# Three extra 128x512 products per round behind the key transposes of a graph-attention pass

## What is computed

```python
def _gat_conv(x, src, dst, W, a_src, a_dst, b, n_nodes):
    h = x @ W
    e = (h @ a_src)[src] + (h @ a_dst)[dst]
    e = jnp.where(e > 0, e, NEG_SLOPE * e)
    w = jnp.exp(e - e_max[dst])
    alpha = w / (denom[dst] + EPS)
    out = jax.ops.segment_sum(alpha[:, None] * h[src], dst, num_segments=n_nodes)
    return out + b
...
for m in range(3):
    x = x + jax.nn.sigmoid(_gat_conv(x, src, dst, Ws[m], att_src[m], att_dst[m], bias[m], n))
```

## Time and profile before

| | us |
|---|---|
| median of 3 runs | 12837.08 |
| lowest and highest of them | 12827.12 and 12846.73 |
| profiled execution, its time | 12854.73 |
| profiled execution, its span | 12853.1 |
| mean granted TensorE clock over the span | 0.735 |

### The profile page before, as it was taken

How to read it: one execution, slowest core, us unless ns; L and a number is a source line. 1 busy time by engine, 2 the same in 40 slices (tenths; PEclk the granted TensorE clock), 3 DMA queues, 4 the chain that set the end, 5 groups by cost and what they waited for, 6 DMA issues and landing times.

```text
span 12853.1 us, 167790 instructions
## 1 busy us (share of the span) xinstructions
PE 7017.4 (55%) x35048; PEld 5096.5 (40%) x35048; DVE 5349.2 (42%) x23215; ACT 4324.3 (34%) x9423; POOL 6444.5 (50%) x5862
## 2 busy tenths in 40 slices
PE   5666666750277007732222377774336887444888
PEld 2333335640266006621111255553224555333666
DVE  5666666651366226643333344441112333111544
ACT  5666663320133005532222244441113444111444
POOL 6666663456555656665666432335663333665000
PEclk9888887875688558855555688985557898555999
DMA  4555554445443555556666665666666777444998
GB/s 154 173 176 172 172 178 121 129 133 189 159 129 127 178 182 167 169 145 157 152 153 153 172 203 202 206 202 173 153 153 190 230 233 224 69 59 87 276 274 270
DMA packets 2016182, 2199.58 MB, mean 171 GB/s; under 512 B 235717, under 2 KB 1404889, under 8 KB 2009712
## 3 DMA queue, kind: packets, MB, share of 16 engines
q1 hardware_dynamic: 1698698, 1822.96, 43.4%
q0 software_dynamic: 308896, 372.55, 14.7%
q10 hardware_dynamic: 8390, 2.21, 0.1%
HBM read 1093.42 MB, written 1119.97 MB: 172 GB/s over the span
## 4 chain that ended last, share of the span: by engine, by line
DMA 18%; issue 11%; PE 10%; DVE 6%; another core or an unknown queue 5%; SPq 3%; POOL 2%; ACT 1%; POOLq 0%; DVEq 0%; ACTq 0%
DMA agg_d<-dO,fOI 11%; PE ps L1407 5%; DMA bXd<-agg_d 4%; PE ps L1394 2%; PE ps L1384 2%; DMA agg_d<-dO,dOI 2%; DMA aX<-y_d 2%; POOL bO L902 1%; SPq L653 1%; DVE aO L2004 1%; DVE uBS L1895 1%; DVE bXd L1977 1%; POOL agg_d L893 1%; PE ps L1382 1%
## 5 line engine op out<-in xcount | busy, mean ns | idle before, releaser
L954 POOL DMA_INDIRECT bXs<-x_d,fGI x784 | 794.7, 1014 | 1546.4 <-DMA x_d<-aH 1334.4
L893 POOL DMA_INDIRECT agg_d<-dO,fOI x784 | 1211.0, 1545 | 648.2 <-ACT dO L1082 417.7
L1082 ACT COPY dO<-ps 128x128 f32<-128x128 f32 (+1 forms) x1176 | 318.2, 271 | 2942.3 <-DMA agg_d<-dO,fOI 1644.7
L1394 PE MATMUL ps<-aS,W1X 128*128 128x512 f32 x2352 | 1206.4, 594 | 0.7 <-DMA eET<-eaT_d 0.7
L1407 PE MATMUL ps<-W,aT 128*128 128x128 f32 x9408 | 1190.3, 288 | 23.2 <-ACT aS L1116 15.9
L2012 DVE TENSOR_TENSOR aH<-ps,B 128x512 f32<-128x512 f32 x588 | 406.4, 692 | 1894.4 <-PE ps L1407 1163.4
L1363 PE MATMUL ps<-bO,bNE 128*128 128x128 f32 x1568 | 577.4, 476 | 1129.5 <-ACT dO L1082 1114.9
L1407 PEld LDWEIGHTS ps<-W,aT 128*128 128x128 f32 x9408 | 1165.6, 205 | 40.1 <-ACT aS L1116 26.3
L1122 ACT ACTIVATE aT<-ps,BNT,BNS 128x512 f32<-128x512 f32 x1176 | 881.3, 774 | 587.7 <-PE ps L1395 556.9
L1181 PE MATMUL ps<-aT,W 128*128 128x512 f32 x1176 | 776.1, 763 | 480.0 <-DVE aT L1570 382.4
L847 POOL DMA_INDIRECT bXs<-x_d,bGI x784 | 785.2, 1001 | 365.7 <-issue 248.2
(11 more groups left out here) (283 smaller groups left out, 17685.3 us busy)
## 6 DMA issues: line engine op xcount, KB each, us to landing
agg_d<-zeros SPq DMA_DIRECT2D x788, 256.0 KB
bXd<-agg_d SPq DMA_DIRECT2D x784, 256.0 KB
agg_d<-zeros SPq DMA_DIRECT2D x394, 290.0 KB
bXd<-agg_d SPq DMA_DIRECT2D x392, 290.0 KB
x_d<-aO SPq DMA_DIRECT2D x392, 256.0 KB
aX<-y_d SPq DMA_DIRECT2D x392, 256.0 KB, 4.0
x_d<-aH SPq DMA_DIRECT2D x392, 256.0 KB
aX<-x_d SPq DMA_DIRECT2D x392, 256.0 KB
```

The costliest lines, as they stand in the source:

```text
L893: pool.indirect_dma_start(agg_d[m][u % 2], bass.IndirectOffsetOnAxis(ap=index, axis=0), dO[:, u, 0:AW[m]], None, bounds_check=agg_last, oo ...
L954: pool.indirect_dma_start(fX[:, s, u, 0:C], None, gin_in[m], bass.IndirectOffsetOnAxis(ap=fGI[:, s, u:u + 1], axis=0), bounds_check=n_last ...
L1394: pe.matmul(z, W1X[:, m, h * P:(h + 1) * P], eHT[:, k, :], start=True, stop=False)
```

## The change

Four lines are added to PE's `p2_round`, behind the key transposes. In each of the 49 rounds of each of the three passes, PE multiplies the identity by 512 columns of `W1X`, three times, into the bank that is not used. Nothing reads the result, no semaphore is waited for or raised, and nothing else is changed.

```diff
--- before
+++ after
@@ -1327,6 +1327,10 @@
                     if inside(i + 2):
                         pe.wait_ge(p_A, U * (r + 2))
                         keys_along(i + 2, s)
+                    if inside(i):
+                        for k in range(3):
+                            pe.matmul(ps[7][:, :], ident[:, :], W1X[:, :, :].rearrange("p m h -> p (m h)")[:, 0:TN],
+                                      start=True, stop=True)
 
                 keys_along(0, 0)
                 pe.wait_ge(p_A, U * (m * R + 1))
```

## The result

| | before | after |
|---|---|---|
| median, runs | 12839.89 us, 4 | 13001.12 us, 4 |
| lowest to highest | 12827.12 to 12846.73 | 12985.96 to 13023.34 |
| profiled execution | 12854.73 us | 12985.96 us |
| pass 0, 1, 2 (first to last scan) | 734.2, 729.4, 716.9 us | 809.6, 808.2, 721.4 us |
| a round, mean | 15.3, 15.2, 14.9 us | 16.9, 16.8, 15.0 us |

The ratio is 1.0128, with a 95% interval of 1.0111 to 1.0146: 161 us slower, where I had forecast 66. The passes grew by 75.4, 78.8 and 4.5 us, 159 us together. The profiled executions differ by 131 us, so other stages, which the change doesn't touch, happened to be 28 us shorter in the one of after.

What follows compares the result with a forecast made beforehand. Rounds were taken as bound by the scatter, a stall behind it, then DVE and ACT, without PE. Terms of 58 + 8 + 0 = 66 us on 12837 gave 12903 us, range 12815 to 13020 us.

Steps and rivals of the forecast that it cites:

- the price of a round of passes 0 and 1: Passes 0 and 1: PE's late second half makes DVE wait, 0.6 us a round, bounds 0 and 2 us; 58 us in all.
- ACT's place: Passes 0 and 1: ACT's second copy must run ahead of the mid-round stall; missing that delays the round, in some rounds only.
- the late rounds of the earlier trace: Pass 0 before the change: two rounds of 16.7 and 16.1 us, 0.8 to 1.4 us above the mean of 15.3.
- First rounds: First and last rounds of each pass: no starvation, PE on the path; 2 to 3 us a pass, 8 us in all.
- PE's slack: Pass 0: PE waits for DVE's scan ahead of L1305 for 35.5 us in 9 rounds, otherwise not at all.
- Clock: Passes 0 and 1: PE's clock rises from 0.83 to about 0.9; added products run cold, the real ones after at full clock.
- Price of the fillers: PE, each round: six added matmuls take 2.6 us at the full clock, 5.1 us at the half clock.
- Pass 2: 0: Pass 2: the layer norm sets the round and PE's wait for the scan or ACT's late copy covers the products; 0 us.
- Signs: Profile after: 882 more matmuls, pass 0 at 763 us, pass 2 unchanged, longer ACT waits at L1064, DVE waiting for L1323.
- All hidden: Rival, chance 0.28: DVE's 11.5 us stall covers PE's lateness in passes 0 and 1; only first rounds cost, 12845 us.
- PE becomes the bound: Rival, chance 0.15: added products run at half clock and rounds of passes 0 and 1 grow by 2 us, 13044 us.
- Faster: Rival, chance 0.12: bridged gaps keep PE's clock at 1.00, ACT copies in time and late rounds shorten; 47 us, 12790 us.

## Why the prediction was right and wrong

- **Direction, and why.** Right. The forecast was slower, through PE arriving late at a scatter, from whose start it runs only about a hundred instructions. The range of 12815 to 13020 us holds the 13001.
- **The size.** The step that failed is the price of a round of passes 0 and 1: "I take 0.6 us, nearest to the late rounds but below them, since not every round will miss ACT's place". The passes show (75.4 + 78.8) / 96 = 1.6 us. Nearly every round missed it. Of the loop's 44 rounds 41 (pass 0) and 43 (pass 1) were late, where it had been 5 and none. I had priced a mixture where one regime came. DVE's wait for ACT's copy, 4.8 us in pass 0 before and 81.0 us after, is the larger part of it. And the late rounds of the earlier trace rows, 0.8 to 1.4 us above the mean, were still too cheap a pattern: with the fillers DVE also waits for PE's last L1323 (31.8 us instead of 4.6), in a stretch where PE is at the half clock (0.50 at 2656). The upper end of 2 us, PE at the half clock behind the stall, was nearer than the value I took.
- **What my bound left out.** I counted the fillers' 12 instructions with PE's time alone. With 36 more, at nearly the same time, the price rose from 161 to 388 us. The hundred instructions that PE runs before it starves are themselves what is spent. What share of the 161 us is due to the number of the first twelve isn't shown: the run with narrow products spends 1.2 us of PE's time a round too.
- **First rounds.** The forecast was 2 to 3 us a pass. The first distance from scan to scan grew from 5.2 to 7.5 us in all three passes.
- **PE's slack.** I wrote that PE waits for the scan in 9 rounds of pass 0 and else not at all. Its weight load has such a wait in 21 of them, 41.9 us in all, but most are of 0.3 us, so the conclusion holds for pass 0. I didn't read pass 1, where PE waited 47.2 us in 19 rounds and had more slack. It paid the same price.
- **Clock.** Forecast about 0.9 in passes 0 and 1: 0.89 and 0.88. The fillers ran at a median of 592 ns, the warm figure. I had put the cold time at the fillers and the full clock at the products after them. It came the other way: the cold stretch lay ahead of them, on L1321 and L1323, for which DVE waits. By the rule of the Trainium skill that I weighed (TensorE: Matmul & The Clock Gate, why this matters for your kernels), filling gaps between bursts keeps the engine fast. The trace agrees on the clock (0.94 in pass 2 with the gap filled, 0.84 before), and it was worth nothing: pass 2 took 712.1 us at 0.95 and 710.2 at 0.84, on the same chip.
- **Price of the fillers.** 2.6 us for six at the full clock; 2.74 us was measured.
- **Pass 2: 0.** It grew by 4.5 us, of which 2.3 us are its first round, within the 10 us I had set. The cover, ACT's late copy, held; with 48 extra instructions it was gone in part of the rounds (820 us).
- **Signs.** ACT's remote waits ahead of L1064 grew, and DVE's multiplications wait 0.85 us for PE's L1323, as forecast. A pass 0 of 763 us was forecast; 809.6 was measured.
- **All hidden (0.28)** is refuted where the stall is present. I argued for it from DVE's own stall of 11.5 us. What defeats it is that PE makes hardly any headway in L1321 and L1323 during that time: 22 instructions in 5.6 us. Beside it I had put a rule (the Trainium skill, Runtime: NRT & Kernel Launch, instruction fetch mechanics): the fetch of straight code is hidden behind issue. No row here speaks against it: the trace lists transfers of instructions on queues of their own, and in the steady part of the loop there are none, though the stall comes all the same (rows below). So the stall may well have another cause, as this rival said. What fell with the counts is its next step, that a late PE starves less.
- **PE becomes the bound (0.15).** Where the stall is present, 1.6 us a round came near the 2 us of this rival, but by another way: PE still idled for 155 of 810 us of pass 0, so it is late at one place and not the bound throughout. Where there is no stall it is literally true, at 0.6 us a round.
- **Faster (0.12)** fell with the order: the fillers follow the starved stretch. Moved ahead of the transposes, they came earlier in over half the rounds of pass 1 alone, and that pass was still longer than before.

DMA traffic of the kernel before, by queue (packets, MB, share of the DMA engines' time), over all of pass 0:

```profile
q1 hardware_dynamic: 105271, 75.50, 34.8%
q0 software_dynamic: 11834, 19.12, 8.0%
q8 instruction: 5, 0.08, 0.0%
q14 instruction: 7, 0.06, 0.0%
```

and from 2130 to 2770 us of it, where these are the only queues:

```profile
q1 hardware_dynamic: 91840, 65.84, 34.7%
q0 software_dynamic: 10439, 16.89, 8.1%
```

The prediction read the starved engines as short of instructions that arrive late beside the scatter. These rows speak against a late transfer: in 640 us of loop no packet of an instruction queue moves, and DVE still has 34 waits with a remote release ahead of L1814 in 40 rounds.

Shown: that the price of the stall hangs on the scatter, that the fillers' price depends on their number as well as their time, that it is about in proportion to the filled rounds, and that the order of ACT isn't the cause. Not shown: what it is in a scatter of eight columns that holds the engines back after about a hundred instructions of PE, and why two chips of the five don't have it. Idle stretches appear on PE, ACT and DVE at once, and none has a releaser that the profile names.

## What to carry over

Before filling an engine's gaps, ask whether the engine is on the ring that sets the round; a higher clock off that ring buys nothing, and the work put there can push the engine onto it. Count instructions as well as time where several engines idle with no releaser while another one issues indirect DMAs: look for how many instructions run from the start of that stretch, and put what must be ready at its end among them. If early and late rounds both occur in a trace, price a delay at the late round in every round, not at a mixture.

## What was not expected of the hardware

- The engines starve in a loop in which no instruction transfer is recorded, so the lack isn't one of the transfers that the trace lists.
- The same program took 11948 us on two chips and 12754 to 12838 us on three others, 7% apart, with rounds of passes 0 and 1 of 10.4 against 15.3 us. A change of 1.3% on one kind was one of 0.3% on the other, by another mechanism.
- Leaving out half of the scatter's columns gave 457 us (3.6%) on a chip with the stall and 57 us (0.5%) on one without.
- One wait more in POOL's program, which delays half of each scatter, made the kernel 1.2% faster on a chip with the stall and no different, or up to 0.2% slower, on one without.
- Pass 2 has a scatter of the same length, but took 710 to 717 us on either kind of chip in the kernels without fillers and with all columns. I read it as its ring through the layer norm hiding the stall; no run tests this.
